# An MoE transformer block on one core: last tile padded with zero rows, second slots matmul moved ahead of the sixth picked tile, expert 0 begun on half its rows, one-hot places built per tile

## The reference

```
h = concat(cls, patches @ W.T + b) + pos_enc          # 32 images x 37 tokens, D = 256
h = h + attn(layernorm(h))                            # causal running sums, low rank R = 64
xf = layernorm(h)                                     # 1184 x 256
gates = softmax(xf @ w_router + b_router)             # 8 experts
topv, topi = top_k(gates, 2)
cap = int(1.25 * n / e)                               # 185 slots per expert
pos = running count of earlier choices of the same expert;  keep = pos < cap
buf[e, pos] = xf[token]                               # gather
out = gelu(buf @ w1[e] + b1[e]) @ w2[e] + b2[e]       # F = 1024
y[token] = sum over its kept choices of gate * out, divided by the sum of its kept gates
h = h + y
```

## Time and profile before

| | |
|---|---|
| median of 3 runs | 162.43 us (162.29 to 164.21) |
| the profiled execution, its own time | 163.64 us |
| its span in the trace | 161.7 us |
| PE busy | 151.7 us (94%) |
| DVE, ACT, POOL busy | 65%, 51%, 31% |
| granted TensorE clock, mean | 0.99 |
| chain that ended last | PE 73%, DMA 10%, DVE 6% |

### The profile page before, as it was taken

How to read it: one execution, slowest core, us unless ns; L and a number is a source line. 1 busy time by engine, 2 the same in 40 slices (tenths; PEclk the granted TensorE clock), 3 DMA queues, 4 the chain that set the end, 5 groups by cost and what they waited for, 6 DMA issues and landing times.

```text
span 161.7 us, 3039 instructions
## 1 busy us (share of the span) xinstructions
PE 151.7 (94%) x1016; PEld 140.4 (87%) x1016; DVE 104.3 (65%) x345; ACT 82.3 (51%) x210; POOL 50.4 (31%) x53
## 2 busy tenths in 40 slices
PE   7989899899999989989999999999999999999950
PEld 7548899798598779879989999999999999999950
DVE  0064957567676799895088858769578596694610
ACT  4122644465307889833626658366573774746200
POOL 4000205004331000001717527267183480703351
PEclk9999999999999999999999999999999999999995
DMA  5999960029402325400189986897879878710422
GB/s 183 394 418 415 401 195 0 0 28 392 152 0 97 101 96 165 149 0 4 53 248 351 282 269 134 284 269 237 268 140 306 258 203 269 167 19 0 51 24 23
DMA packets 17123, 28.48 MB, mean 176 GB/s; under 512 B 1149, under 2 KB 13607, under 8 KB 16857
## 3 DMA queue, kind: packets, MB, share of 16 engines
q1 hardware_dynamic: 14649, 25.49, 45.8%
q0 software_dynamic: 2464, 2.86, 10.0%
HBM read 24.21 MB, written 4.14 MB: 175 GB/s over the span
## 4 chain that ended last, share of the span: by engine, by line
PE 73%; DMA 10%; DVE 6%; issue 2%; ACT 2%; POOL 2%; SPq 2%; POOLq 1%; ACTq 0%
PE ps L1270 23%; PE ps L1293 12%; DMA cst<-const 8%; PE ps L1121 7%; PE ps L1295 5%; PE ps L1101 4%; PE ps L1174 4%; PE ps L1279 3%; PE ps L1231 3%; DMA out_rows<-out_s,dst_row 2%; PE ps L1204 2%; PE ps L1189 2%; POOL out_rows L495 2%; PE ps L1303 2%; PE ps L1217 2%
## 5 line engine op out<-in xcount | busy, mean ns | idle before, releaser
L495 POOL DMA_INDIRECT out_rows<-out_s,dst_row x16 | 23.8, 1485 | 38.3 <-ACT out_s L672 31.9
L648 ACT ACTIVATE first_t<-ps,b_cur 128x186 f32<-128x186 f32 x64 | 23.1, 413 | 24.3 <-PE ps L1270 24.3
L1293 PE MATMUL ps<-hid_hl,split 128*128 128x372 f32 x96 | 29.0, 369 | 0.0
L1295 PE MATMUL ps<-hid_hl,split 128*128 128x186 f32 x96 | 23.9, 248 | 0.0
L1270 PE MATMUL ps<-first_t,w_even 128*128 128x186 f32 x128 | 21.8, 322 | 0.7 <-ACT first_t L520 0.7
L1270 PE MATMUL ps<-first_t,patch_t 128*128 128x186 f32 x128 | 21.7, 322 | 0.1
L1270 PEld LDWEIGHTS ps<-first_t,w_even 128*128 128x128 f32 x128 | 20.1, 190 | 1.0 <-issue 1.0
L965 DVE CAST hid_hl<-first_t 128x372 fp32r<-128x372 f32 x28 | 10.7, 383 | 15.8 <-ACT first_t L648 15.8
L1270 PEld LDWEIGHTS ps<-first_t,patch_t 128*128 128x128 f32 x128 | 20.1, 190 | 0.4 <-issue 0.4
L480 POOL DMA_INDIRECT rows_in<-xrows,src_row x14 | 15.8, 1130 | 11.8 <-DVE src_row L933 7.8
L1295 PEld LDWEIGHTS ps<-hid_hl,split 128*128 128x128 f32 x96 | 18.3, 191 | 0.0
(11 more groups left out here) (174 smaller groups left out, 265.5 us busy)
## 6 DMA issues: line engine op xcount, KB each, us to landing
w_even<-w SPq DMA_DIRECT2D x8, 1024.0 KB, 5.7
patch_t<-w SPq DMA_DIRECT2D x8, 1024.0 KB, 5.2
att<-attn SPq DMA_DIRECT2D x1, 1280.0 KB, 9.8
patch_t<-patches SPq DMA_DIRECT2D x1, 1080.0 KB, 12.0
first_t<-first SPq DMA_DIRECT2D x1, 978.0 KB, 7.4
out_rows<-h SPq DMA_DIRECT2D x2, 384.0 KB, 2.5
xrows<-xn SPq DMA_DIRECT2D x2, 384.0 KB, 2.8
patch_t<-patches SPq DMA_DIRECT2D x1, 756.0 KB, 13.4
```

The lines of the kernel that those rows point to most:

```text
L495: pool.indirect_dma_start(out=out[:, :], out_offset=bass.IndirectOffsetOnAxis(ap=dst_row[0:SIZES[s], c:c + 1], axis=0), in_=out_s[q][0:SIZ ...
L648: ins = act.activation(hid[:, f, :], bank(pair)[:, (f % 2) * SL:(f % 2 + 1) * SL], ACT.Gelu, bias=b1_cur[q][:, f:f + 1])
L1293: pe.matmul(dst[:, 0:2 * SL], w2_h[q][:, f, cols], hid_hl[:, f].rearrange("p a s -> p (a s)"), start=f == 0, stop=False)
L1295: ins = pe.matmul(dst[:, 0:SL], w2_l[q][:, f, cols], hid_hl[:, f, 0], start=False, stop=f == KF - 1)
```

## The change

What it does, part by part:

1. Last tile. POOL sets tile 9 of `xn` and of `at_p` to zero early (two more memsets), and `pick`, `xn_t` and `look_up` now multiply all 128 rows of tile 9, of which 96 are zero. ACT and PE wait for the memsets (`pool_set` 9 and 10).
2. `slots` part 1 stands on PE ahead of the pick of tile 5 (HELD = 1) and not behind it. The three spare products of `keep_warm` are gone.
3. Expert 0 starts when half 0 of its rows is copied. `up_first` multiplies half 0 of blocks 0 and 2, then half 1 of both, then blocks 1 and 3. ACT's copy of half 1 stands ahead of its `row_marks`, where it stood behind it. `look_up` stands behind all 16 `up` products of expert 0, where it stood behind 14.
4. `find_slots` builds `at_p` with one tensor_tensor for up to two tiles and both choices, where it took one tensor_scalar for each tile and choice; the input is the float32 table, and `iota_b` is gone. `take_in` of expert 0 stands ahead of `find_slots(0, 2)`. For tile 9 only its 32 rows are written.
5. `know` is one reduction over all tiles, behind `count` part 1, where there were two.
6. `set_prefix` (now `neg_prefix` alone) stands behind `patches_low` of group C, where it stood ahead of that of group B.

The diff, cut: `grid` and `spread` get a number of partitions as last argument, the tile `iota_b` is no longer allocated, and DVE_ORDER only loses its last two steps, ("know", 0) and ("know", 1).

```diff
@@ -26,3 +26,3 @@
 GROUPS = [(0, 3), (3, 3), (6, 2), (8, 2)]
-KEEP_WARM = 3
+HELD = 1
 BRIDGES = {('slots', 0): 4, ('pick', 0): 3}
...
@@ -454,2 +453,4 @@
             pool.memset(wr_c[:, :, NE:], 1.0 / D).then_inc(pool_set, 1)
+            pool.memset(xn[:, NT - 1], 0.0).then_inc(pool_set, 1)
+            pool.memset(at_p[:, NT - 1], 0.0).then_inc(pool_set, 1)
 
@@ -615,2 +616,4 @@
                 elif kind == "norm1":
+                    if n == E:
+                        act.wait_ge(pool_set, 9)
                     act.wait_ge(stats1_ready, nth(DVE_ORDER, ("rstd1",), ("rstd1", n)))
@@ -639,2 +642,5 @@
 
+            act.wait_ge(picked, KD)
+            copy(buf_t[0][:, 1:], pick_slot[:, 1:]).then_inc(half_ready, 1)
+
             act.wait_ge(places_known, 1)
@@ -675,4 +681,2 @@
 
-            act.wait_ge(picked, KD)
-            copy(buf_t[0][:, 1:], pick_slot[:, 1:]).then_inc(half_ready, 1)
             for pair in range(PAIRS):
@@ -762,3 +766,2 @@
                 dve.wait_ge(const_in, 16)
-                dve.tensor_copy(iota_b[:, :], iota_slot[:, 0:ST])
                 dve.tensor_copy(neg_prefix[:, :], cst[0:TT, C_NEG]).then_inc(prepared, 1)
@@ -817,7 +820,6 @@
 
-            def know(g):
+            def know():
 
-                ts = slice(CHOICES[g][0], sum(CHOICES[g]))
-                drained(dve, "slots", g)
-                dve.tensor_reduce(slot_of[:, ts], by_expert[:, ts], AX.X, ALU.add).then_inc(slots_known, 1)
+                drained(dve, "slots", len(CHOICES) - 1)
+                dve.tensor_reduce(slot_of[:, :], by_expert[:, :], AX.X, ALU.add).then_inc(slots_known, 1)
 
@@ -857,3 +859,2 @@
                 if kind == "uw":
-                    set_prefix()
                     patches_low(SPLIT[0])
@@ -865,2 +866,3 @@
                     patches_low(SPLIT[1])
+                    set_prefix()
                 elif kind == "proj":
@@ -899,4 +901,2 @@
                                       ).then_inc(below_ready, 1)
-                elif kind == "know":
-                    know(n)
 
@@ -914,5 +914,8 @@
 
-                for t in range(a, b):
-                    for k in range(2):
-                        dve.tensor_scalar(at_p[:, t, k], iota_b[:, :], slot_p[:, t, k:k + 1], None, ALU.is_equal)
+                if b == NT:
+                    dve.wait_ge(pool_set, 10)
+                for r, i, j in tile_parts(a, b):
+                    if i < j:
+                        dve.tensor_tensor(at_p[0:r, i:j], grid(iota_slot[0:r, 0:ST], j - i, 2, ST, r),
+                                          spread(slot_p[0:r, i:j], j - i, ST, r), ALU.is_equal)
 
@@ -989,3 +992,4 @@
 
-            dve.wait_ge(slots_known, len(CHOICES))
+            know()
+            dve.wait_ge(slots_known, 1)
             dve.tensor_scalar(upper[:, :, :], slot_of[:, :, :], float(ST), None, ALU.is_ge)
@@ -1007,4 +1011,4 @@
             m = marked(dve.scalar_tensor_tensor(got[:, :], every[:, :], 1e-6, got[:, :], ALU.mult, ALU.max))
-            find_slots(0, 2)
             take_in(0, 0, first=True)
+            find_slots(0, 2)
             behind(m)
@@ -1081,6 +1085,6 @@
                 pe.wait_ge(rows_marked, 1)
+                pe.wait_ge(pool_set, 10)
                 for t in range(NT):
-                    r = rows_of(t)
                     for k in range(2):
-                        ins = pe.matmul(dst, at_p[0:r, t, k, :], marks[0:r, t, k].rearrange("p c q -> p (c q)"),
+                        ins = pe.matmul(dst, at_p[:, t, k, :], marks[:, t, k].rearrange("p c q -> p (c q)"),
                                         start=t + k == 0, stop=t == NT - 1 and k == 1)
@@ -1091,22 +1095,19 @@
                 t0, c = CHOICES[g]
-                last = t0 + c == NT
-                for halves in ([[k] for k in range(KD)] if last else [range(KD)]):
-                    for t in range(t0, t0 + c):
-                        for m, (first, _n) in enumerate(GROUPS):
-                            if t == first:
-                                done(pe, ("rows2", m))
-                        pe.wait_ge(onehot_ready, t + 1)
-                        r = rows_of(t)
-                        for k in halves:
-                            ins = pe.matmul(pick_slot[:, k, :], xn[0:r, t, k * 128:(k + 1) * 128],
-                                            onehot[0:r, t, :], start=t == 0, stop=t == NT - 1)
-                    if last:
-                        ins.then_inc(picked, 1)
-
-            def keep_warm(products):
+                if g == 0:
+                    pick_tiles(range(t0, t0 + c - HELD), range(KD))
+                    return
+                pick_tiles(range(t0 - HELD, t0), range(KD))
+                for k in range(KD):
+                    pick_tiles(range(t0, t0 + c), [k]).then_inc(picked, 1)
 
-                drained(pe, "norm2", E)
-                spare = slot("norm2", E)[:, 512:640]
-                for _ in range(products):
-                    pe.matmul(spare, mean_mat[:, :], mean_mat[:, :], start=True, stop=True)
+            def pick_tiles(tiles, halves):
+                for t in tiles:
+                    for m, (first, _n) in enumerate(GROUPS):
+                        if t == first:
+                            done(pe, ("rows2", m))
+                    pe.wait_ge(onehot_ready, t + 1)
+                    for k in halves:
+                        ins = pe.matmul(pick_slot[:, k, :], xn[:, t, k * 128:(k + 1) * 128], onehot[:, t, :],
+                                        start=t == 0, stop=t == NT - 1)
+                return ins
 
@@ -1213,7 +1214,8 @@
                     t0, c = GROUPS[n]
+                    if n == E:
+                        pe.wait_ge(pool_set, 9)
                     for i in range(c):
-                        r = rows_of(t0 + i)
                         for k in range(KD):
-                            ins = pe.transpose(p[:, k * 512 + i * TT:k * 512 + i * TT + r],
-                                               xn[0:r, t0 + i, k * 128:(k + 1) * 128], ident[0:r, 0:r])
+                            ins = pe.transpose(p[:, k * 512 + i * TT:k * 512 + (i + 1) * TT],
+                                               xn[:, t0 + i, k * 128:(k + 1) * 128], ident)
                 elif kind == "zc":
@@ -1250,4 +1252,2 @@
                 ins.then_inc(psum_filled, 1)
-                if (kind, n) == ("slots", 1):
-                    keep_warm(KEEP_WARM)
 
@@ -1261,3 +1261,3 @@
 
-            def up(e, q, pair, reused, blocks=(0, 1)):
+            def up(e, q, pair, reused):
                 if pair == 0:
@@ -1267,3 +1267,3 @@
                     pe.wait_ge(hid_ready, (e - 1) * PAIRS + pair + 1)
-                for f in (2 * pair + i for i in blocks):
+                for f in (2 * pair, 2 * pair + 1):
                     for k in range(KD):
@@ -1271,4 +1271,16 @@
                                         buf_t[q][:, k, :], start=k == 0, stop=k == KD - 1)
-                if blocks[-1] == 1:
-                    ins.then_inc(up_done, 1)
+                ins.then_inc(up_done, 1)
+
+            def up_first():
+
+                pe.wait_ge(w1_in[0], 16)
+                for k, f in ((0, 0), (0, 2), (1, 0), (1, 2), (0, 1), (1, 1), (0, 3), (1, 3)):
+                    if (k, f) == (0, 0):
+                        pe.wait_ge(buf_ready, 1)
+                    if (k, f) == (1, 0):
+                        pe.wait_ge(half_ready, 1)
+                    ins = pe.matmul(bank(f // 2)[:, (f % 2) * SL:(f % 2 + 1) * SL], w1_s[0][:, k, f * 128:(f + 1) * 128],
+                                    buf_t[0][:, k, :], start=k == 0, stop=k == KD - 1)
+                    if k == KD - 1 and f % 2:
+                        ins.then_inc(up_done, 1)
 
@@ -1323,14 +1335,12 @@
             def expert(e, q, first=False, last=False):
-                up(e, q, 0, not first)
-                if not first:
+                if first:
+                    up_first()
+                else:
+                    up(e, q, 0, True)
                     turn_out(e - 1)
-                for pair in range(1, PAIRS - 1):
+                for pair in range(2 if first else 1, PAIRS - 1):
                     up(e, q, pair, not first)
+                up(e, q, PAIRS - 1, not first)
                 if first:
-                    up(e, q, PAIRS - 1, False, blocks=(0,))
                     look_up(bank(MARKS_BANK)[0:ST, 0:(ID_PARTS + PARTS) * SC])
-                    up(e, q, PAIRS - 1, False, blocks=(1,))
-                else:
-                    up(e, q, PAIRS - 1, True)
-                if first:
                     pe.wait_ge(w2_in[q], 8 * (e - q) + 16)
@@ -1354,3 +1364,2 @@
             drained(pe, "slots", len(CHOICES) - 1)
-            pe.wait_ge(half_ready, 1)
             expert(0, 0, first=True)
```

23 lines of the change are left out of this document (11 added, 12 removed).

## The result

| | before | after |
|---|---|---|
| median | 162.59 us (162.21 to 164.21, 22 runs) | 162.12 us (161.17 to 162.62, 22 runs) |
| the profiled execution, its own time | 163.64 us | 162.62 us |
| its span in the trace | 161.7 us | 160.8 us |
| PE busy | 151.7 us | 151.3 us |
| granted TensorE clock, mean | 0.99 | 0.99 |

A forecast was written before the change was run, and what follows sets the result against it. PE was taken to bound the kernel nearly throughout, except at the front, routing and expert 1's gather. Terms -0.47 + 0.15 - 0.1 - 1.4 = -1.8 gave 161.8 us for the profiled execution, 160.6 by the median; range 159.9 to 161.9.

The forecast's parts named there:

- the term -0.47: Front: with set_prefix moved, PE starts the projection when it is free, at 17.25 instead of 17.72, saving 0.47 us.
- The cast's new price of +0.15: DVE, behind group C's last low part: the moved neg_prefix cast delays group A's statistics, costing 0.15 us (bounds 0.1 and 0.21).
- The two rivals with the cast behind POOL (23% and 5%): neg_prefix cast waits for one POOL m_l (161.3 us, 23%) or all three (162.8 us, 5%).
- -0.1: xn_t of tile 9: full-row products save two changes of form but transposes grow, 0.1 us gained (bounds 0 and -0.4).
- 0.73 for three changes of form: Pick of tiles 6 to 9: three changes between 128-row and 32-row tiles cost 0.24 us each, all removed by zero rows.
- The rival "zero rows bring nothing": Changes of form in pick, look_up and xn_t cost 0, the 0.73 has another source: -1.25, or 161.2 us; 8%.
- forecast -1.35: Routing: up of expert 0 starts at 68.85, 1.35 us earlier, with DVE's take_in, not the pick, ending last.
- the gather ends last by a little: Ahead of turn_in: expert 1's gathered rows come 4.54 us behind look_up, at 79.54, just later than PE at 79.42.
- the sentence "From there PE works through experts 1 to 7 without a gap, and loads and copies are issued by PE's progress, so the shift reaches the end.": Behind expert 1's turn_in: the whole 1.4 us gained from the pick on was to reach the kernel's end.
- New gaps among experts 1 to 7: Sign of a wrong forecast: PE showing new gaps in experts 1 to 7, where none were expected.
- the forecast 1.8: Whole kernel: 1.8 us faster, 161.8 for the profiled execution and 160.6 by the median; 48%.
- the 4% for something unseen: Whole kernel: chance left for an outcome covered by neither the forecast nor any rival, with no size given; 4%.

The follow-up runs named there:

- a_zeroback: Changed kernel, but pick, xn_t and look_up again multiply only the 32 real rows of tile 9; one run, 161.63 us.
- a_again: The changed kernel run again unchanged: 161.97 us, ratio to the kernel before 0.9917.
- b_again: The kernel before run again unchanged: 162.8 us, ratio 1.0.
- The pair with both mends: Changed kernel and kernel before, each with expert 2's w2 loaded ahead of w1 and twelve spare PE products ahead of slots part 0: 161.08 and 162.68 us.

## Why the prediction was wrong

**Front.** The wait that the term -0.47 was read from is 0.41 on average over five profiles of the old front, so the size was nearly right, but that is luck in part: it varies from 0 to 0.71 with the arrival of the constants (14.6 to 15.8) and with PE's own start, and I had read it from one. Its cause held: DVE's work behind POOL's copy made the low part late, and with the cast moved away PE never waits here. The cast's new price of +0.15 came as forecast, and DVE was ahead of POOL, by 0.02. The two rivals with the cast behind POOL (23% and 5%) did not happen.

**Zero rows.** `xn_t` gave -0.22 where I took -0.1: from group A's `xn_t` to `chosen` it is 30.10 and not 30.32, and with the old rows 30.32 again (a_zeroback). In the pick, where I had taken 0.73 for three changes of form, they are worth 0.58: 20 instructions of PE's line 1112 take 4.19 in the timeline of a_zeroback,

```profile
63.45 4.19 PE L1112 MATMUL ps<-onehot,xn 128*128 128x186 f32 x20
```

and 3.61 in that of the changed kernel,

```profile
64.59 3.61 PE L1110 MATMUL ps<-onehot,xn 128*128 128x186 f32 x20
```

of which 0.24 reaches `up` (the rest is hidden by DVE). The rival "zero rows bring nothing" falls. By the sentence of the Trainium skill, "TensorE: Matmul & The Clock Gate", "Step-by-step: what each phase is for", that the row count does not matter, the two rows would be alike; the measurement decides against it as a rule for a sequence that changes between 128 and 32 rows. The same skill's "TensorEngine Tiling (Array Packing)", "Key Properties", says that a change of tiling mode drains the engine, and that agrees.

**Routing and gather.** From `chosen` to `up` 9.07 instead of 10.48: -1.41, forecast -1.35. `up` waits for DVE's copy with 0.14 behind its end, as written. From `up` to `turn_in` 10.77, and the rows come 4.54 behind `look_up` (74.66 to 79.20), as in the kernel before; the gather ends last by a little, as forecast. All this held, to within 0.1. Beneath it, `look_up` took 0.91 where I had 0.82.

**From there to the end.** The step that failed is the sentence "From there PE works through experts 1 to 7 without a gap, and loads and copies are issued by PE's progress, so the shift reaches the end." The loads of expert 2 are not issued by PE's progress alone. SP stands in its queue behind the load that waits for the gathered rows, and only then asks for w1 and w2. The two loads in the kernel before:

```profile
81.13 0.41 SPq L393 DMA_DIRECT2D w_even<-w  x1
82.16 0.40 SPq L396 DMA_DIRECT2D w_even<-w  x1
```

There w1 is asked for 0.16 behind `turn_in` (which starts at 80.97), in the changed kernel 0.68 (79.91 to 79.23). For w2 it is 1.19 and 1.29. The pair takes its time from the first of the two: w2 lands 8.4 to 8.5 behind the issue of w1 in the kernel before and 8.1 to 8.7 in the changed one. So w2 came later against PE: its split began 8.86 behind `turn_in`, in a_again 9.40, in b_again 8.68. Since nothing was to spare, each tenth that PE came earlier and the load did not was lost. Over the nine profiles of the changed kernel with this load order unmended, the stretch is 13.35 to 13.92; in the three of the kernel before it is 13.09, 13.20 and 13.27. That is 0.4 on average.

My own sums had this difference in them. By them `look_up`, and with it the gather and everything behind it in SP's queue, came 0.88 earlier, but `up` 1.35 and `turn_in` 1.4, because two products had moved from behind `look_up` to ahead of it. Only the smaller shift belongs to the loads. The earlier trace rows and the chain behind it show SP and PE reaching this place within 0.7 us of each other, and I followed PE only. New gaps among experts 1 to 7 stood in the prediction as a sign of being wrong; this is one.

**Behind PE.** 6.20 and 6.01 against 5.74 and 5.67, for the instruction fetch that meets the scatter: 0 to 0.5 by the stretches, 0 to 0.45 by the medians. I had not thought of it; nothing in the argument spoke of the length of PE's program.

Put together: -1.41 - 0.22 + 0.15 - 0.41 is -1.89 at `turn_in`, close to the forecast 1.8; 0.4 lost at `turn_out` and 0 to 0.45 behind PE leave -1.0 to -1.5. Measured were 0.82 (0.5 to 1.2) and 1.35 (0.8 to 1.9) by the two ratios, so the sum agrees with the second and is at the edge of the first; some tenths may be open there. The pair with both mends, 1.60 apart, is also 0.3 short of 1.89; the late loads of experts 3 and 4 are a likely part of that, but one profile each cannot show how often they occur. Neither the forecast nor any rival had the case "the shift is lost later"; only the 4% for something unseen were left for it.

## What to carry to other kernels

When a stage gets shorter, follow each load behind it, not only PE: write down when its issue moves and what stands ahead of it in its queue. A load that landed just in time turns into the new wait as soon as its consumer moves further than its issue, and when it is mended, the next one may. Of two loads asked in succession, the one that is needed first by a tight margin goes first, and a gather on the critical path should have the DMA queues to itself. And judge a wait that hangs on the arrival of a DMA from several executions: here it was 0, 0.24, 0.47, 0.61 and 0.71.
